# Moving routing work and weight loads in a mixture-of-experts kernel: table rows, router order, ring loads, combines

## What is computed

```
aff = sigmoid(x @ wa)                        # 2048 tokens, 16 experts
topk_p, topk_i = top_k(aff, 2)               # two experts per token
topk_p = topk_p / sum(topk_p)
expert(x) = (gelu(x @ g + gb) * (x @ w1 + b1)) @ w2 + b2     # 512 -> 256 -> 512
out = x + sum of 2 shared experts(x) + topk_p[0]*expert_a(x) + topk_p[1]*expert_b(x)
x = x + gb * out
```

## Time and profile before

| what | value |
| --- | --- |
| median of 3 runs | 1423.64 us (1423.6 to 1424.46) |
| the profiled execution, its own time | 1421.54 us |
| its span, first to last instruction | 1419.7 us |
| TensorE busy | 1357.7 us, 96% of the span |
| VectorE, ScalarE, GpSimd busy | 858.7, 670.4, 381.8 us |
| mean granted TensorE clock | 0.985 |

### The profile page before, as it was taken

One profiled execution on the slowest core, in us unless ns is written; L12 is line 12 of the kernel. 1 busy time (PEld: TensorE's weight loads), 2 busy tenths in 40 slices (PEclk: granted clock), 3 DMA queues, 4 the chain that ended last, 5 costly groups with the idle time before them and its releaser, 6 DMA issues. The chain is left out here.

```text
span 1419.7 us, 23230 instructions
## 1 busy us (share of the span) xinstructions
PE 1357.7 (96%) x7092; PEld 1140.3 (80%) x7092; DVE 858.7 (60%) x1761; ACT 670.4 (47%) x1551; POOL 381.8 (27%) x339
## 2 busy tenths in 40 slices
PE   6899998999999999999999999998998999989997
PEld 3666777888888888888888888886776888868885
DVE  5786754655666666666776566665574434434568
ACT  3333326666666666666666666662312223222232
POOL 0334453000003091030640123700042233322262
PEclk9999999999999999999999999998998999999998
DMA  9999877966677669685799766874635789887374
GB/s 294 374 388 339 299 282 270 361 202 228 200 269 266 224 226 321 207 318 196 269 365 368 244 225 196 295 292 174 248 127 200 280 304 331 304 329 258 128 241 136
DMA packets 160042, 375.59 MB, mean 265 GB/s; under 512 B 23144, under 2 KB 80556, under 8 KB 147680
## 3 DMA queue, kind: packets, MB, share of 16 engines
q1 hardware_dynamic: 144432, 314.34, 63.1%
q0 software_dynamic: 15536, 60.30, 11.9%
HBM read 245.84 MB, written 128.22 MB: 263 GB/s over the span
## 5 line engine op out<-in xcount | busy, mean ns | idle before, releaser
L1155 ACT ACTIVATE a_pr<-a_pr,a_stat 128x128 f32<-128x128 f32 (+3 forms) x256 | 142.0, 556 | 113.8 <-DVE a_stat L1226 113.5
L1326 PEld LDWEIGHTS a_psY<-a_pT,a_cv 128*128 128x128 f32 x768 | 124.9, 190 | 15.9 <-issue 2.1
L1226 DVE CUSTOM_DVE_ANT_0 a_pr<-a_psS,f_mask 128x128 f32<-128x128 f32 (+3 forms) x256 | 114.6, 487 | 31.4 <-PE a_psS L1314 31.0
L1326 PE MATMUL a_psY<-a_pT,a_cv 128*128 128x512 f32 (+3 forms) x768 | 131.2, 320 | 1.9 <-DVE a_pT L1245 1.9
L1161 ACT ACTIVATE a_pr<-a_pr,a_stat 128x128 f32<-128x128 f32 (+3 forms) x256 | 122.2, 548 | 0.0
L1171 ACT ACTIVATE a_oT<-a_psY 128x512 fp32r<-128x512 f32 x64 | 38.2, 598 | 151.0 <-PE a_psY L1326 151.0
L1256 DVE TENSOR_TENSOR n_acc<-a_psZ,n_acc 128x512 f32<-128x512 f32 x125 | 86.4, 691 | 35.2 <-PE a_psZ L104 33.0
L1240 DVE TENSOR_TENSOR a_oT<-a_psY,a_oT 128x512 fp32r<-128x512 f32 x64 | 44.2, 691 | 103.7 <-ACT a_oT L1171 103.7
L102 PE MATMUL a_psX<-a_hT,a_wqk 128*128 128x512 f32 (+1 forms) x256 | 100.3, 392 | 0.6 <-DVEq L1216 0.6
L103 PE MATMUL a_psX<-a_hT,a_wqk 128*128 128x512 f32 (+1 forms) x256 | 100.4, 392 | 0.0
L104 PE MATMUL a_psX<-a_hT,a_wqk 128*128 128x512 f32 (+1 forms) x256 | 100.1, 391 | 0.0
(11 more groups left out here) (354 smaller groups left out, 3469.6 us busy)
## 6 DMA issues: line engine op xcount, KB each, us to landing
w1s_d<-a_ws SPq DMA_DIRECT2D x72, 512.0 KB, 3.5
a_wqk<-wqk_d SPq DMA_DIRECT2D x64, 512.0 KB, 4.6
a_mh<-mhl_d SPq DMA_DIRECT2D x32, 1024.0 KB, 6.2
s_ring<-w1s_d SPq DMA_DIRECT2D x16, 2048.0 KB, 9.4
w2s_d<-a_ws SPq DMA_DIRECT2D x72, 256.0 KB, 4.0
qpe_d<-p_qs SPq DMA_DIRECT2D x16, 1024.0 KB, 5.1
a_rw<-in_L_ffn_rw SPq DMA_DIRECT2D x128, 128.0 KB, 3.5
a_qpe<-qpe_d SPq DMA_DIRECT2D x64, 256.0 KB, 2.7
```

The source lines that it names most:

```text
L1155: nc.scalar.activation(pr[i], pr[i], ACT.Exp, bias=nmax[:, i:i + 1], scale=-1.0, accum_out=rsum[:, i:i + 1]).then_inc(ex, 1)
L1226: nc.vector.tensor_tensor_reduce(out=pr[i], in0=score[i][:, 0:w], in1=mask[:, S - w:S], scale=-1.0, scalar=3e38, op0=ALU.add, op1=ALU.min, ...
L1326: m = nc.tensor.matmul(psY[:, q0:S], cv[:, j, cs], pT[:, ps, o:o + w], start=n == 0, stop=n == 11)
```

## The change

Four parts, all in `stage_ffn`.

1. `NP` goes from 18 to 13: POOL makes 13 rows and DVE 19. DVE's order becomes: `ranked` ahead of `update(0, 3)`; seven rows ahead of `times(1, 1)`, twelve behind it; `tables` behind `times(1, 2)`.
2. On PE `router(LAST)` moves up between the two parts of `first_two(0)`, ahead of the last products of batch 0's tiles 0 and 1, and `by_token(LAST)` ahead of `second(0, 2)`.
3. On SP the 2 MB load of an expert waits for `fo` in place of `oo`, and only the 1 MB load still waits for `oo`.
4. At the end the tiles are dealt out differently: tile 0 after slice 1, tile 1 after slice 2, tiles 2 to 8 after slice 3 of `LAST`; then 9, 10, 11 behind slices 0, 1, 2 of batch 2, tile 15's `combine` behind slice 3, then 12, 13, 14, and `finish([15])`. Tiles 8 to 14 are combined by `whole`, four operations: the shared result is added from PSUM before the multiplication with the gate.

```diff
-    NP = 18
+    NP = 13
...
-        tiles_m = {LAST: [[], [], [0], [1, 2]], 2: [[11], [12], [13], [14]]}
+        tiles_m = {LAST: [[], [0], [1], [2, 3, 4, 5, 6, 7, 8]], 2: [[9], [10], [11], [15]]}
...
-                    sp.wait_ge(oo, sp.value_load(lead[0:1, bass.ds(e - 2, 1)], min_val=1, max_val=NBLK))
+                    done = sp.value_load(lead[0:1, bass.ds(e - 2, 1)], min_val=1, max_val=NBLK)
+                    sp.wait_ge(fo, done)
                     sp.sem_inc(step_p, 1)
                     sp.dma_start(ring1[:, s].rearrange("p c s n -> p (c s n)").bitcast(F32),
                                  K.w1s_d[bass.ds(e, 1)].rearrange("a p c s n -> (a p) (c s n)")).then_inc(rw1_in[s], 16)
+                    sp.wait_ge(oo, done)
                     sp.dma_start(ring2[:, s].rearrange("p f s n -> p (f s n)").bitcast(F32),
...
                     for i in tiles_m[LAST][m]:
                         scaled(i)
-                for i in range(3, 11):
-                    scaled(i)
                 for m in range(NU):
                     gelu(2, m)
                     y_high(2, m)
-                    for i in tiles_m[2][m]:
-                        scaled(i)
-                scaled(15)
+                    if m < NU - 1:
+                        scaled(9 + m)
+                for i in range(12, 16):
+                    scaled(i)
...
                 update(0, 2)
+                ranked()
                 update(0, 3)
                 times(1, 0)
                 y_low(1, 0)
-                ranked()
                 counts()
                 blocks_of()
+                last_spots(range(NP, 20))
                 times(1, 1)
                 y_low(1, 1)
-                last_spots(range(NP, 25))
-                tables()
+                last_spots(range(20, TOP * NT))
                 times(1, 2)
                 y_low(1, 2)
-                last_spots(range(25, TOP * NT))
+                tables()
                 times(1, 3)
                 y_low(1, 3)
                 tokens()
...
-                dve.wait_ge(g4_in, 16 * B)
-                dve.wait_ge(base3, 1)
+                def whole(i):
+
+                    n, b, t = done[0], turns[i] // TB, turns[i] % TB
+                    a = at[:, i % NA]
+                    dve.wait_ge(a_ok, i + 1)
+                    v.scalar_tensor_tensor(out=a, in0=got[i % NG][:, i % (NG // 2) * TOP + 1], scalar=wt[:, 1, turns[i]:turns[i] + 1],
+                                           in1=a, op0=ALU.mult, op1=ALU.add).then_inc(cch, 1)
+                    dve.wait_ge(sh_o, place_of[b] * TB + t + 1)
+                    dve.wait_ge(cch, n + 1)
+                    tt_(a, final[b][t], a, ALU.add).then_inc(cch, 1)
+                    dve.wait_ge(cch, n + 2)
+                    tt_(a, a, gb4[:, b], ALU.mult).then_inc(cch, 1)
+                    dve.wait_ge(cch, n + 3)
+                    if b in s_in:
+                        dve.wait_ge(s_in[b], 16)
+                    tt_(a, a, total[b][:, t], ALU.add).then_inc(o_ok, 1)
+                    done[0] = n + 3
+
                 for m in range(NU):
                     times(LAST, m)
                     y_low(LAST, m)
-                    combine(tiles_m[LAST][m])
-                for i in range(3, TB + TB):
-                    combine([i])
-                combine([8], True)
-                finish([8])
...
-                finish([10])
+                    if m == 1:
+                        dve.wait_ge(g4_in, 16 * B)
+                        dve.wait_ge(base3, 1)
+                    for i in tiles_m[LAST][m]:
+                        if i < 2 * TB:
+                            combine([i])
+                        else:
+                            whole(i)
                 for m in range(NU):
                     times(2, m)
                     y_low(2, m)
-                    combine(tiles_m[2][m], True)
-                    if m == 0:
-                        finish([11])
-                combine([15], True)
-                for i in range(12, 16):
-                    finish([i])
+                    for i in tiles_m[2][m]:
+                        if m < NU - 1:
+                            whole(i)
+                        else:
+                            combine([i], True)
+                for i in range(12, 15):
+                    whole(i)
+                finish([15])
...
-                first_two(0, lambda: by_token(2))
-                router(LAST)
+                def last_logits():
+                    by_token(2)
+                    router(LAST)
+
+                first_two(0, last_logits)
+                by_token(LAST)
                 second(0, 2)
-                by_token(LAST)
                 second(0, 3)
```

More of the change, by code:

```diff
@@ L2062, in _ @@
                     y_low(LAST, m)
-                    combine(tiles_m[LAST][m])
-                for i in range(3, TB + TB):
-                    combine([i])
-                combine([8], True)
-                finish([8])
-                combine([9], True)
-                finish([9])
-                combine([10], True)
-                finish([10])
+                    if m == 1:
[6 more added lines that the diff above has]
+                            whole(i)
                 for m in range(NU):
```

## The result

The changed kernel takes 1405.91 us (median of 4 runs, 1402.25 to 1406.21) against 1423.62 (4 runs, 1418.05 to 1424.46): a ratio of 0.987, 95% interval 0.9847 to 0.9894. Of the 17.7, 2.4 come from which execution was profiled: that of before stood 2.1 under its median, that of after (1406.2) stands 0.3 over. The two profiled executions differ by 15.3, and that is what the traces can explain.

A forecast was written before the change was run, and what follows sets the result against it. TensorE, busy 96% of the span, was taken to bound the kernel, along with other engines finishing after it at the end. Gains of 3.3 (routing), 5.7 (weights) and 2.1 (end) sum to 11.1: 1423.64 becomes 1412.5 us, range 1408 to 1418.5.

The forecast's parts named there:

- Routing: Ahead of the first expert block: tokens copied 4.8 us earlier, less 1.5 for a clock fall, gaining 3.3 us.
- an indirect load 1 us quicker: Gather of block 0's rows: upper bound of 5.8 us, as neighbouring 2 MB and 1 MB loads start 5 to 7 earlier.
- The copy: Routing's end on VectorE: the tokens are copied at 1070.8 against 1075.57, 4.8 us earlier.
- VectorE's walk: Routing: VectorE's queue stepped through in its new order with old operation lengths, from ranks at 1042.1 to tokens at 1070.8.
- The clock: Behind the gap for block 0's rows: some 3 us of products at half speed, costing 1.5 us; bounds 0 and 4.
- the rival that the clock holds: Before the first block: the 3.5 us gap passes without a clock fall, giving 1411.0 us; chance 0.25.
- Weights: Expert blocks: loads requested 6.8 us earlier remove TensorE's waits of 2.48 and 3.23 at experts 13 and 14, gaining 5.7.
- the loads' pace eats the lead: Expert blocks: the earlier request does not bring later loads forward; 1418.2 with nothing won, 1415.4 with half; chance 0.15.
- The end: Last tiles: 6.44 us of TensorE idle goes, then the gather for tile 15 binds; gain 2.1, bounds 0.2, 2.9 and 5.5.
- The end gives nothing: Last tiles: tile 15's late gather holds back tiles 12 to 14, 2.1 us less gain, 1414.6; chance 0.08.
- Slower: Weight loads: the 1 MB load no longer overlaps the 2 MB one, each expert exceeds 14.43 us; some 1430; chance 0.03.
- the rival that they block: Routing: seven VectorE rows each wait 0.98 for a GpSimd row, so routing gives -1.7, time 1417.5; chance 0.04.

The follow-up runs named there:

- w2_late: The changed kernel with expert 0's 1 MB load asked for only once block 0's rows have landed; 1401.97 us, one run.
- undo_router: The changed kernel with TensorE's old order put back, the router's products of the last batch where they were; 1408.06 us, one run.
- undo_routing: The changed kernel with parts 1 and 2 undone: 18 rows on GpSimd, old orders on VectorE and TensorE; 1412.23 us, 0.9915 of before.
- end_split: The changed kernel with second shares of tiles 12, 13, 14 first and tile 15's held back until tile 13 is finished; 1403.84 us, one run.
- tokens_first: The changed kernel with the copy of the tokens one slice earlier, ahead of batch 1's last `times` and `y_low`; 1406.29 us, one run.
- undo_end: The changed kernel with part 4 undone, the tiles dealt out as before; 1409.95 us, 0.9908 of before.
- best1: The changed kernel with end_split, w2_late's wait, tokens_first and the block table read one tile earlier on TensorE; 1401.11 us, 0.9849 of before.
- best2: best1 with the 1 MB load behind block 1's rows and the mark for expert 0's 2 MB load ahead of that wait; 1401.76 us, 0.9846 of before.
- only_routing: The kernel before with parts 1 and 2 alone, weight loads and end old; 1417.64 us, one run.

## Why the prediction was wrong in its size

The direction and the three places stood, and one step of the mechanism failed: the gather was carried over at its old time. The forecast, 1412.5, was 6.6 us too high, and the measured 1405.9 lies below the range. 2.4 of the 6.6 is where the two profiled executions stand to their medians (2.1 + 0.3), 0.2 is the earlier S of after, and 4.0 is the sum of the terms, 15.1 against 11.1: 2.7 in the routing, 0.8 in the blocks, 0.5 at the end. With the 4.0 and the 0.2 alone the time would have been 1408.3, just inside the range of 1408 to 1418.5, so it took the scatter as well to leave it.

- **Routing, 3.3, measured 6.0** (5.3 to 8.0 over the six executions with this routing). The step that failed is "The token path is later: from copy to TensorE it was 8.05 us ... now 1070.8 + 8.05 = 1078.85. So the stall on the rows does not go, it grows from 1.3 to some 3.5 us". The 8.05 was not a constant of the gather: it holds a 1 MB load that was asked for 0.5 us ahead of it. The change left that load where the last product puts it and the copy behind slice 3, so they came 2.4 apart, and copy to use took 6.54: 1.5 of the 2.7 us. w2_late shows the cause: with the load behind them the rows land in 3.4 us, against 5.9 in after. I had this as a bound (5.8, "an indirect load 1 us quicker") and took the other end.
- **The copy, 1070.8, measured 1069.50.** Counted from S it came 1.1 us earlier than forecast, which is the rest of the 2.7 but for 0.1. This is VectorE's walk. The twelve rows took 3.17 and not 3.5, and `tables` 4.9 (1062.55 to 1067.44) and not 5.6. Both old lengths were read while GpSimd made its rows, and the change moved `tables` and most of the twelve rows behind them: beside GpSimd VectorE's rows come 0.29 us apart and the small operations of `tables` take up to twice as long (last section). Old lengths were carried over here too, past a neighbour that was gone.
- **The copy's release.** In before the copy followed TensorE's last small product at once; VectorE stood idle for 3.11 us ahead of it. In after the last product was done 1.95 us before the copy, which waited for slice 3. So what held the tokens changed from TensorE to VectorE's own queue.
- **Part 2, 0.4 to 0.5 (TensorE's wait at `order`), measured 0.40** by undo_router's trace.
- **The clock, -1.5, measured -1.3 to -1.6** where it falls. It fell in four executions of six, so the rival that the clock holds is as live as the forecast. That the term fits is partly luck: I had it from a gap of 3.5 us, and the gap was 1.54.
- **Weights, 5.7, measured 6.5.** The mechanism stood, request 6.7 us ahead and both gaps gone. The idle time was the wrong measure of their price: 5.71 of idle cost the blocks 6.46. The margin was as thin as said: undo_routing, end_split, tokens_first and w2_late, all with part 3 in, had one gap each, of 2.05, 1.61, 1.45 and 0.60, so the rival "the loads' pace eats the lead" comes true in part in some executions (the loads of experts 3 to 14 stood 14.3 to 14.6 us apart in the runs with part 3, before had 14.43). Expert 3's 1 MB load comes 6.7 late and takes about 0.9 us of the lead at once.
- **The end, 2.1, measured 2.6** (undo_end: 3.4). VectorE waits 3.62 ahead of tile 15 (walk: 3.5), released by ScalarE. That fit is partly luck. Tile 8's four operations after 1378.7 end at 1381.5 and not at 1382.4, and 1382.5 + 16.7 is 1399.2 and not 1399.5: VectorE came to tile 15 0.8 us earlier than the walk has it, counted from O, and the gather some 0.7 earlier. It was asked for 55.3 us behind O, and 56.5 in before: the row of gathers ran 1.1 us earlier, a part of the bound of 5.5, and the last landed 0.4 later than the 4.1 of the earlier trace rows. "The end gives nothing" is out.
- **Slower** is out: the loads' pace stood, 14.3 us per expert against 14.43, with the 1 MB load behind a wait of its own.
- **VectorE's rows beside GpSimd.** Its seven rows took 2.04 in both kernels, so charging nothing was right, and the rival that they block is out.

## What to carry to other kernels

A measured time from request to use holds whatever else was in flight: before it is carried over as a constant, look at what was asked for in the last few microseconds before it and whether the change moves the two apart. The same goes for an operation's length beside a busy neighbour. A bulk load that can wait a few microseconds for a small gather is worth moving behind it, as long as the loads that follow in its queue do not lose their lead by it. When the last result waits for a transfer, put work that doesn't need it first, and don't give the late tile the first place.

## What the runs showed of the hardware

- A gather of block 0's rows, with a 2 MB load asked for 5.7 to 5.9 us ahead, landed in 3.4 us (w2_late), in 5.6 to 6.0 with a 1 MB load asked for 2.4 ahead as well, and in 7.4 to 7.7 with that 0.5 ahead. With the 2 MB load 3.9 ahead and no 1 MB load it took 5.3 (best1) and 5.7 (best2).
- GpSimd's rows, by their line in after, are 786 ns at the least, 840 in the median and 1952 at the most:

```profile
L1649 POOL TENSOR_SCALAR s_hx<-n_rows,n_t x13: 786/840/1952, 1045.0 to 1057.3; 128x128 fp32r<-128x128 f32 x13
```

  The longest starts at 1052.1, beside VectorE's two comparisons of two inputs (its timeline):

```profile
1051.66 1.83 DVE L1880 TENSOR_TENSOR s_ring<-n_t,n_rows 128x768 fp32r<-128x768 f32 x2
```

  The Trainium skill, "SBUF — State Buffer", section "SBUF: two separate sides", says that a VectorE operation with two SBUF inputs and a GpSimd operation that reads SBUF exclude each other for a whole instruction. That row took 1.16 us more than the shortest, and the comparisons end at 1053.5, 1.4 us behind its start: as an estimate from these rows, the trace agrees, if not to the last 0.2 us. VectorE's own rows, of one tensor input, were not blocked: they came 0.29 us apart beside GpSimd's (seven in 2.04) and 0.26 apart mostly without them (twelve in 3.17). The small operations of `tables` did feel it: L1902 took 0.41 in undo_routing, inside GpSimd's rows, and 0.21 in after, behind them.
- The same code ahead of the stage ended anywhere in 6 us (975.4 in best2, 981.3 in undo_router), 0.4% of the kernel's time, so that two single executions of equal kernels can differ by as much as one of these parts is worth.
- A stall of TensorE for a weight load cost 0.3 to 0.7 us beyond its idle time, and 2.5 more where the clock fell behind it for 6.7 us (only_routing).
